# Moving one subtraction to GpSimd, three state copies to VectorE, and the gate's input ahead of the recurrence's output

## The reference, cut to what matters

```python
xn = layernorm(x)
r_in, k_in, v_in = (xn * mix + prev_xn * (1 - mix) for mix in (mix_r, mix_k, mix_v))
receptance, key, value = r_in @ Wr.T, k_in @ Wk.T, v_in @ Wv.T
# for each token t, in order, per channel, with w = -exp(time_decay), u = time_first:
mo = max(m, key + u);  e1 = exp(m - mo);  e2 = exp(key + u - mo)
wkv = (e1 * num + e2 * value) / (e1 * den + e2)
ms = max(m + w, key);  e1s = exp(m + w - ms);  e2s = exp(key - ms)
num, den, m = e1s * num + e2s * value, e1s * den + e2s, ms
# and then
rwkv = sigmoid(receptance) * wkv
s = rwkv @ Wo.T
g = silu(relu(xn @ W1 + b1) @ W2 + b2)
x = x + s * g
```

## Time and profile before

| | |
|---|---|
| time, median of 3 runs | 2056.8 us (2056.05 to 2057.78) |
| the profiled execution | 2056.05 us, its span 2054.2 us |
| PE busy | 1902.8 us, 93% of the span |
| DVE busy | 1719.4 us, 84% |
| ACT busy | 1734.6 us, 84% |
| POOL busy | 565.9 us, 28% |

### The profile page before, as it was taken

One profiled execution on the slowest core, in us unless ns is written; L12 is line 12 of the kernel. 1 busy time (PEld: TensorE's weight loads), 2 busy tenths in 40 slices (PEclk: granted clock), 3 DMA queues, 4 the chain that ended last, 5 costly groups with the idle time before them and its releaser, 6 DMA issues. The chain is left out here.

```text
span 2054.2 us, 53386 instructions
## 1 busy us (share of the span) xinstructions
PE 1902.8 (93%) x22950; PEld 975.5 (47%) x22950; DVE 1719.4 (84%) x2241; ACT 1734.6 (84%) x2169; POOL 565.9 (28%) x418
## 2 busy tenths in 40 slices
PE   3999999999994998998999999999999999999986
PEld 1565655655553555555444434444344444344445
DVE  5999999999896777776788888888888888888876
ACT  5767777677765778777999999999999999999971
POOL 0654655646544556655000000000000000000018
PEclk9999999999997999999899999999999999999999
DMA  3001001010112455558222222222222222222139
GB/s 106 21 22 42 21 22 42 22 42 21 53 42 77 135 180 175 171 180 219 73 58 67 68 72 71 63 65 67 68 72 73 56 68 55 53 61 58 56 100 319
DMA packets 130220, 166.24 MB, mean 81 GB/s; under 512 B 13632, under 2 KB 101696, under 8 KB 129728
## 3 DMA queue, kind: packets, MB, share of 16 engines
q1 hardware_dynamic: 127952, 160.59, 26.4%
q10 hardware_dynamic: 2032, 2.24, 0.3%
HBM read 91.21 MB, written 71.57 MB: 79 GB/s over the span
## 5 line engine op out<-in xcount | busy, mean ns | idle before, releaser
L1748 ACT ACTIVATE c_probs<-c_ps_b 128x1536 f32<-128x1536 f32 x544 | 888.4, 1633 | 0.0
L1862 PE MATMUL c_ps_o<-c_probs,c_v 128*32 128x256 f32 (+3 forms) x6656 | 582.2, 453 | 3.9 <-DVE c_probs L1780 0.8
L1780 DVE TENSOR_SCALAR c_probs<-c_probs 128x2048 f32<-128x2048 f32 (+2 forms) x415 | 434.1, 1056 | 68.1 <-ACT c_probs L1748 67.7
L1842 PE MATMUL c_ps_b<-c_qk 24*128 24x256 f16 (+2 forms) x8064 | 459.8, 294 | 4.5 <-PEq L1089 4.5
L1842 PE MATMUL c_ps_a<-c_qk 24*128 24x256 f16 (+2 forms) x2688 | 449.8, 294 | 6.8 <-ACT c_probs L1747 5.2
L1747 ACT ACTIVATE c_probs<-c_ps_a 128x512 f32<-128x512 f32 x544 | 419.2, 771 | 2.4 <-PE c_ps_a L1842 2.4
L1842 PEld LDWEIGHTS c_ps_b<-c_qk 24*128 24x128 f16 x8064 | 222.7, 93 | 331.4 <-ACT c_probs L1748 243.9
L2009 POOL TENSOR_TENSOR d_prod<-d_prod,d_x 128x1024 f32<-128x1024 f32 x8 | 26.2, 3291 | 1022.0 <-DVE d_prod L1997 1022.0
L1862 PEld LDWEIGHTS c_ps_o<-c_probs,c_v 128*32 128x32 f32 x6656 | 161.7, 109 | 245.8 <-issue 126.9
L278 POOL TENSOR_TENSOR a_hidh<-a_hid,a_hidh 128x512 f16<-128x512 f32 x128 | 205.1, 1631 | 135.2 <-ACT a_hidh L403 134.0
L1785 DVE TENSOR_SCALAR c_probs<-c_probs 128x1536 f32<-128x1536 f32 (+2 forms) x208 | 165.8, 804 | 54.9 <-ACT c_probs L1748 52.7
(11 more groups left out here) (270 smaller groups left out, 2778.3 us busy)
## 6 DMA issues: line engine op xcount, KB each, us to landing
v_d<-b_val SPq DMA_DIRECT2D x16, 1024.0 KB
c_v<-v_d SPq DMA_DIRECT2D x64, 256.0 KB
rows<-in_x SPq DMA_DIRECT2D x16, 512.0 KB, 5.0
x_d<-rows_out SPq DMA_DIRECT2D x16, 512.0 KB, 3.2
rows<-x_d SPq DMA_DIRECT2D x16, 512.0 KB, 5.0
qc_d<-b_qc SPq DMA_DIRECT2D x16, 512.0 KB
kc_d<-b_kc SPq DMA_DIRECT2D x16, 512.0 KB
gate_d<-rows_out SPq DMA_DIRECT2D x16, 512.0 KB, 3.3
```

Of the source, the lines that this page charges most:

```text
L1748: nc.scalar.activation(probs[:, t % NPROB, PARTS[1]], ps_b[:, t % 2], ACT.Exp, scale=unscale).then_inc(exp_b_done, 1)
L1780: nc.vector.tensor_scalar(tile, tile, P_MAX, P_MIN, ALU.min, ALU.max).then_inc(clip_done, 1)
L1842: mm = nc.tensor.matmul(into, k[rows, hk, kt * P:(kt + 1) * P], tokens[rows, hq], start=(i == 0), stop=(i == len(TERMS) - 1), tile_positio ...
L1862: mm = nc.tensor.matmul(ps_o[j * VW:(j + 1) * VW, column:column + w], v[:, kt, j * VW:(j + 1) * VW], probs[:, step % NPROB, j, at:at + w], ...
```

## The change

Four edits. DVE's subtraction for `rwkv_half[1]` is deleted and stands on POOL, in `rwkv_low_of`, first in the turn of the body, ahead of `silu`. In all turns but the last, DVE's `gate_input` goes ahead of the multiplication that makes `rwkv`, and ACT's `gate_sigmoid` ahead of the copy into `rwkv_half[0]`. `old_states` leaves ACT for DVE, behind the statistics of chunk `n + 3`, and for chunk 0 directly ahead of `keys(0)`; at a sequence's start it uses three memsets where it copied from constants, so that POOL's constant `mx_start` is gone.

```diff
@@ POOL
-                pool.memset(mx_start[:], MAX_INIT).then_inc(consts_set, 1)
-                pool.wait_ge(consts_set, 6)
+                pool.wait_ge(consts_set, 5)
...
+                def rwkv_low_of(n):
+                    pool.wait_ge(rwkv_high, n + 1)
+                    nc.gpsimd.tensor_tensor(rwkv_half[:, 1], rwkv[:], rwkv_half[:, 0], ALU.subtract).then_inc(rwkv_low, 1)
+
...
                     n = count(b, c)
+                    rwkv_low_of(n)
                     silu(n)
@@ ACT
-                def old_states(n, c):
-
-                    act.wait_ge(num_done, n + 1)
-                    act.wait_ge(consts_set, 6)
-                    for t, start in ((mx, mx_start[:]), (num, zero_col[:, 0:KT]), (den, zero_col[:, 0:KT])):
-                        before = t[:, :, CH:CH + 1] if c % CPB else start
-                        nc.scalar.activation(t[:, :, 0:1], before, ACT.Copy).then_inc(state_set, 1)
-
...
                     receptance(n)
-                    old_states(n, c)
...
                     n = count(b, c)
+                    if left >= 1:
+                        gate_sigmoid(n)
                     act.wait_ge(rwkv_done, n + 1 + 1)
                     act.wait_ge(out_done, n + 1)
                     nc.scalar.activation(rwkv_half[:, 0], rwkv[:], ACT.Copy).then_inc(rwkv_high, 1)
-                    gate_sigmoid(n)
+                    if left == 0:
+                        gate_sigmoid(n)
@@ DVE
+                def old_states(n, c):
+
+                    dve.wait_ge(num_done, n + 1)
+                    if c % CPB == 0:
+                        nc.vector.memset(mx[:, :, 0:1], MAX_INIT).then_inc(state_set, 1)
+                        nc.vector.memset(num[:, :, 0:1], 0.0).then_inc(state_set, 1)
+                        nc.vector.memset(den[:, :, 0:1], 0.0).then_inc(state_set, 1)
+                    else:
+                        for t in (mx, num, den):
+                            nc.vector.tensor_copy(t[:, :, 0:1], t[:, :, CH:CH + 1]).then_inc(state_set, 1)
...
                 weight_low(3)
+                old_states(0, 0)
                 dve.wait_ge(consts_done, 1)
                 keys(0)
...
                     n = count(b, c)
+                    if left >= 1:
+                        gate_input(n)
+
                     dve.wait_ge(q_done, n + 1 + 1)
                     dve.wait_ge(rden_done, 2 * n + 2)
 
                     nc.vector.tensor_tensor(rwkv[:], out_num[:], out_den[:], ALU.mult).then_inc(rwkv_done, 1)
-                    gate_input(n)
-                    dve.wait_ge(rwkv_high, n + 1)
-                    nc.vector.tensor_tensor(rwkv_half[:, 1], rwkv[:], rwkv_half[:, 0], ALU.subtract).then_inc(rwkv_low, 1)
+                    if left == 0:
+                        gate_input(n)
                     if left >= 3:
                         layernorm(n + 3, c + 3, b + (c + 3) // X)
                         dve.wait_ge(stats_done, TPC * (n + 3) + TPC)
+                    if left >= 1:
+                        old_states(n + 1, c + 1)
```

More of the change, by code:

```diff
@@ L80, in layer0 @@
         zero_col = sb("a_zero", [P, 2 * KT, 1])
-        mx_start = sb("a_mx_start", [P, KT, 1])
         eps = sb("a_eps", [P, TPC])
```

## The result

The changed kernel takes 2092.62 us (median of 4, 2091.72 to 2093.38), the kernel before, on the same chip, 2056.68 us: a ratio of 1.0174 (95% interval 1.0158 to 1.0190), some 36 us slower. I had forecast 28 us slower, with a range that holds the measured time. On the path that I followed, the starts in an undisturbed chunk came out within 0.2 us of those worked out. What I had only as a rival, PE's falling clock, came true in 8 of the 15 chunks. It costs 13.3 us, more than the 8 us by which the forecast fell short.

The account below looks back on a forecast made before the run. The bound was taken as a ring through DVE whose last wait, ahead of `prod`, is the gate's chain. 15 chunks x (1.68 + 0.20) + 1.2 - 1.5 = 27.9 us slower, so 2084.7 us; range 2073 to 2107.

Parts of the forecast that it names:

- PE's falling clock: Rival, chance 0.10: idling 2.7 us ahead of the output product slows PE, 1.47 us in each of 15 chunks, 2106.8 us.
- The ring and its last wait: Loop: `rwkv` multiplication, other engines, `prod`, 29.66 us of DVE, next multiplication; the gate's chain through POOL's `silu` releases `prod` last.
- The step of 1.68 us a chunk: Gate first plus a 2.30 us subtraction on POOL delay PE's output product; `prod` starts at 8.86 instead of 7.18.
- The follow-on waits: Key product and first exponential come late after `prod` in each loop chunk: +0.2 us, 0 to 0.6.
- rival on POOL and DVE hindering each other: Chance 0.05: POOL's subtraction takes 3.34 us, +1.04 in each of 15 chunks, 2100.3 us.
- signs of being wrong: `prod` at 7.2 after DVE's chunk start, output product over 4 us, or DVE's 29.66 us stretch shorter by more than 1.
- the case in which the clock holds: Likeliest case, chance 0.70: PE's clock stays up, 2084.7 us, own range 2076 to 2093.
- The old states: Three two-column operations on DVE, about 0.1 us each, inside its gap of some 4.4 us ahead of `prod`: no effect.
- The start: `keys(0)` no longer waits 4.25 us for ACT's copies: -1.5 us once, bounds -0.3 and -1.8.
- The last chunk: Old order kept on DVE and ACT, but POOL's slower subtraction stays: +1.2 us once.
- DVE's relief pays: Rival, chance 0.05: DVE's work sets the loop's period, so less of it gives -14.1 us, 2042.7 us.
- The waits between POOL and DVE: Rival, chance 0.04: the two `mixed_low` subtractions on DVE shrink, giving back 1.9 us a chunk; 2056.8 +- 4 us.

Follow-up runs that it names:

- silu_first: The changed kernel with POOL's two operations swapped, `silu` ahead of the subtraction: 2122.74 us, 1.0315 of the kernel before.
- old_states_alone: The kernel before with only the old states moved from ACT to DVE: 2053.82 us, 0.9981.
- pe_filled: The changed kernel with 20 extra products on PE per turn but the last, ahead of its wait for the low half: 2079.35 us, 1.0104 of the kernel before.
- low_on_dve: The changed kernel with the subtraction back on DVE, gate first and old states on DVE kept: 2096.64 us, 1.0187 of the kernel before.
- low_on_pool_alone: The kernel before with only the subtraction moved to POOL, ahead of `silu`: 2065.13 us, 1.0035.
- silu_waits: The changed kernel with the subtraction back on DVE and POOL's `silu` waiting for it: 2065.53 us, 1.0044 of the kernel before.
- gate_first_alone: The kernel before with only `gate_input` and `gate_sigmoid` moved ahead, in all turns but the last: 2101.05 us, 1.0208.

## Why the prediction was right, and where it was short

**The ring and its last wait: right.** With the table load taken out of the gate's chain `prod` moved 0.65 us forward; with the subtraction 1.1 us later on POOL the output product moved with it (silu_first). The 29.66 us behind `prod` are less firm than I took them: 29.81 in the changed kernel, 29.37 in old_states_alone.

**The step of 1.68 us a chunk: right in its sum, measured 1.47.** Each handover held. POOL's subtraction took 2.12 us in all 16 chunks, less than twice the shortest row of the half size; 2.30 was 0.18 too much. The follow-on waits were 0.15 a chunk (0.20 forecast), so 1.62 in all.

**What I did not see in this step.** I priced the two edits in one chain and named the subtraction as its heading. The experiments put the weight elsewhere: the order of the gate alone costs 43 us, the subtraction on POOL alone 7 to 8. Once the gate is first, having the subtraction on POOL rather helps, since it can then not meet `silu`: in the traces a fast chunk takes 38.46 us against 38.64, and 8 chunks are slow against 9. The times, 2092.6 and 2096.6, point the same way, though the intervals of the two ratios overlap. On DVE it would meet it, and I had expected 2065 for that kernel. My rival on POOL and DVE hindering each other had the mechanism, but looked at the subtraction on POOL only.

**PE's clock: the step that was mis-sized.** The sum put it at nothing and the rival at 22 us for all 15 chunks, chance 0.10. Measured: 8 of 15 chunks, 1.66 each, 13.3 us; pe_filled gives them back. That is why the result is 2092.6 and not about 2080. An output product over 4 us was one of my own signs of being wrong, and in 8 chunks it came. That the measured time still lies inside 2076 to 2093, the range of the case in which the clock holds, is in part luck: all other terms came out 4 us lower in sum than forecast, and this hid a third of the 13.3 us.

**The old states: right in the changed kernel's sum, wrong in their price.** I gave them 0.1 us each and a gap of 4.4 us; two of three waited for POOL for about 2 us each, and 0.35 us of the gap was left. I had named that wait and its cover until 8.86, and the cover held.

**The start: -1.5 forecast, -1.9 measured.** L569, which multiplies the new values, waited for ACT's exponential until 54.46, as worked out (54.7).

**The last chunk: +1.2 forecast, +2.0 measured**, since the output product there started 0.94 us later against L688 and took 5.3 instead of 4.25 us, behind 4.68 us of idling. The length of the idling does not explain the duration: behind 3.75 us the same product took 5.30 in low_on_dve and 4.25 in the kernel before.

**DVE's relief pays: refuted** by low_on_pool_alone, where the relief became idle time. The waits between POOL and DVE did not shrink either: DVE's two subtractions in `mixed_low` (L511, in the kernel before L514) take 5.06 us together in a chunk, against 2 x 2.52.

## What to carry to other kernels

Follow the ring in time and not the shares: an operation taken from a busy engine gains nothing if that engine idles right behind it. If an edit moves an operation with two inputs on DVE or POOL, look at what the other of the two does in that instant, tiny copies included, and let the one off the path wait. And if an edit lengthens PE's idle time by a microsecond or two, count its clock as a term of the sum, not as a remote case; here taking a table load out of the chain was worth more than any move between engines.

## What was not expected of the hardware

- How often PE was slow behind an idle stretch was higher where the stretch was longer; these are counts of single traces, and the kernels differ in their period too. With 1.3 us (low_on_pool_alone) and 1.56 us (silu_waits) no output product of the loop was slow, with 2.50 us 8 of 15 (the changed kernel), with 2.67 us 9 of 15 (low_on_dve) and 10 of 15 (gate_first_alone), with 3.7 us 15 of 15 (silu_first).
- DVE's copy of two columns, 0.15 us by itself, took up to 2.33 us beside POOL's operations with two inputs, and the middle one of three slipped in between two of these.
- An added wait made a kernel some 30 us faster (silu_waits against low_on_dve).
